# Attention scores as four matmuls of 32 weight columns instead of one of 128, on one core of a Trainium2 chip

## The reference

```python
x = x + ln(attn(ln(x)))                 # 16 heads of 8 features, with a TISA bias
x = x + ln(ffn(ln(x)))                  # msa without bias, then a mixture of 8 experts
# attn: logits = (q @ k.T) / sqrt(8) + bias[head, i - j]; softmax over j; @ v
# ffn:  x = x + msa(ln1(x)) @ w_proj; x = x + expert(argmax gate)(ln2(x))
```

## Time and profile before

| | |
|---|---|
| median of three executions | 914.77 us (913.09 to 916.9) |
| span of the profiled execution | 917.8 us |
| TensorE (PE) matmuls, busy | 810.0 us (88%), 8,629 records |
| weight loads (PEld), busy | 302.8 us (33%), 8,629 records |
| VectorE (DVE), busy | 752.3 us (82%) |
| ScalarE (ACT), busy | 636.7 us (69%) |
| GpSimd (POOL), busy | 242.1 us (26%) |
| scores_a, line 1266 | 1,024 matmuls, mean 394 ns, together 327.5 us busy |
| scores_b, line 1305 | 1,024 matmuls, mean 387 ns, together 333.7 us busy |

### The profile page before, as it was taken

How to read it: one execution, slowest core, us unless ns; L and a number is a source line. 1 busy time by engine, 2 the same in 40 slices (tenths; PEclk the granted TensorE clock), 3 DMA queues, 4 the chain that set the end, 5 groups by cost and what they waited for, 6 DMA issues and landing times.

```text
span 917.8 us, 22092 instructions
## 1 busy us (share of the span) xinstructions
PE 810.0 (88%) x8629; PEld 302.8 (33%) x8629; DVE 752.3 (82%) x1196; ACT 636.7 (69%) x1266; POOL 242.1 (26%) x548
## 2 busy tenths in 40 slices
PE   4269999999999999999999999999999999954960
PEld 2013333333333333343232223322232322344950
DVE  5469978899999998879899998899999899336734
ACT  6027777777777777777678989899988899921311
POOL 4010413201000415222300533333011301004773
PEclk9559999999999999999999999999999999976985
DMA  3654444565555455355313333242322121001313
GB/s 98 186 170 154 133 161 141 157 199 174 171 173 162 142 164 170 125 168 174 100 54 100 109 113 98 65 126 79 93 59 54 54 85 52 28 18 48 52 49 100
DMA packets 69469, 104.67 MB, mean 114 GB/s; under 512 B 15845, under 2 KB 45861, under 8 KB 69365
## 3 DMA queue, kind: packets, MB, share of 16 engines
q1 hardware_dynamic: 62805, 68.31, 25.7%
q10 hardware_dynamic: 5088, 31.92, 10.0%
q0 software_dynamic: 1472, 3.02, 1.5%
HBM read 84.19 MB, written 18.87 MB: 112 GB/s over the span
## 4 chain that ended last, share of the span: by engine, by line
PE 67%; DVE 10%; POOL 6%; DMA 5%; issue 4%; ACT 4%; SPq 3%; ACTq 0%; POOLq 0%; DVEq 0%
PE bank L1286 23%; PE bank L1305 20%; PE bank L1312 11%; PE bank L1266 7%; DVE unit_max L1003 4%; ACT prob_mem L901 3%; POOL prob_mem L791 3%; POOL moe_out L797 2%; DMA maxima_rows<-max_rows 2%; PE bank L1349 2%; PE bank L1239 1%; DVE no_use L999 1%; DVE stats L946 1%; PE bank L1234 1%; DMA k_parts<-prob_mem 1%
## 5 line engine op out<-in xcount | busy, mean ns | idle before, releaser
L901 ACT ACTIVATE prob_mem<-bank 128x512 f32<-128x512 f32 x1024 | 556.6, 597 | 149.3 <-PE bank L1312 124.0
L1266 PE MATMUL bank<-k_rows,q_rows 56*128 56x512 bf16 x1024 | 327.5, 394 | 22.6 <-DMA k_rows<-k_parts 12.3
L1305 PE MATMUL bank<-q_rows,k_rows 59*128 59x512 bf16 x1024 | 333.7, 387 | 12.0 <-DMA k_rows<-k_parts 5.3
L999 DVE CUSTOM_DVE_ANT_1 no_use<-bank,w_moe 128x1024 bf16<-128x1024 f32 x256 | 305.5, 1218 | 37.6 <-PE bank L1266 33.4
L1286 PE MATMUL bank<-prob_mem,v_ring 128*32 128x256 f32 x4096 | 322.2, 388 | 7.7 <-issue 6.6
L1003 DVE TENSOR_REDUCE unit_max<-bank 128x1 f32<-128x1024 f32 x256 | 297.5, 1215 | 19.7 <-PE bank L1266 18.1
L702 POOL CAST max_parts<-unit_max 128x8 bf16<-128x8 f32 x64 | 12.1, 189 | 568.5 <-DVE unit_max L999 321.0
L1305 PEld LDWEIGHTS bank<-q_rows,k_rows 59*128 59x128 bf16 x1024 | 80.8, 93 | 244.0 <-issue 114.7
L1286 PEld LDWEIGHTS bank<-prob_mem,v_ring 128*32 128x32 f32 x4096 | 103.0, 109 | 153.5 <-ACT prob_mem L901 61.8
L1312 PE MATMUL bank<-skew_mem,pick 96*32 96x512 bf16 x1664 | 138.7, 390 | 0.0
L1010 DVE TENSOR_TENSOR bank<-bank,w_moe 128x512 f32<-128x512 f32 x96 | 67.0, 698 | 26.0 <-PE bank L1305 25.8
(11 more groups left out here) (177 smaller groups left out, 525.0 us busy)
## 6 DMA issues: line engine op xcount, KB each, us to landing
w_moe<-bias_rows ACTq DMA_DIRECT2D x31, 960.0 KB, 5.7
q_rows<-q_parts SPq DMA_DIRECT2D x252, 48.0 KB
k_rows<-k_parts SPq DMA_DIRECT2D x126, 96.0 KB
skew_mem<-bias_parts SPq DMA_DIRECT2D x32, 378.0 KB, 4.9
unit_sums<-o_ring SPq DMA_DIRECT2D x63, 128.0 KB, 2.4
w_moe<-in_L_ffn_w_dram SPq DMA_DIRECT2D x16, 256.0 KB, 3.1
q_parts<-prob_mem SPq DMA_DIRECT2D x8, 384.0 KB, 3.1
k_parts<-prob_mem SPq DMA_DIRECT2D x24, 128.0 KB, 2.8
```

The lines of the kernel that those rows point to most:

```text
L901: nc.scalar.activation(prob[:, kb, half * N:(half + 1) * N], b_bank(("exp", exp_no(n, kb, half))), ACT.Exp).then_inc(exp_done, 1)
L999: nc.vector.tensor_tensor_reduce(out=no_use[:, qb % 2, :].rearrange("p (k c) -> p k c", k=QB), in0=scores.rearrange("p (k c) -> p k c", k= ...
L1266: return nc.tensor.matmul(sa_slot(QB * m + qb)[:, f, :], q_rows[rows, m % SLOTS, qb * P:(qb + 1) * P], k_rows[rows, m % SLOTS, f * N:(f + ...
L1305: return nc.tensor.matmul(b_bank(("exp", exp_no(n, kb, f))), k_rows[rows, n % SLOTS, kb * P:(kb + 1) * P], q_rows[rows, n % SLOTS, f * N:( ...
```

## The change

Both score functions loop over four groups of 32 weight columns. Each group has its own matmul, which writes 32 partitions of the same bank and is placed at the tile position (64 f, 32 c). The moving operand is the same 512 columns for all four. Waits and increments stay on the first and last instruction of a half; the order, the banks and the values computed stay.

```diff
--- before.py
+++ after.py
@@ -1263,8 +1263,12 @@
             def scores_a(m, qb, f):
 
                 rows = slice(f * HP, f * HP + KR)
-                return nc.tensor.matmul(sa_slot(QB * m + qb)[:, f, :], q_rows[rows, m % SLOTS, qb * P:(qb + 1) * P],
-                                        k_rows[rows, m % SLOTS, f * N:(f + 1) * N], start=True, stop=True)
+                for c in range(4):
+                    at = qb * P + VM * c
+                    ins = nc.tensor.matmul(sa_slot(QB * m + qb)[VM * c:VM * (c + 1), f, :], q_rows[rows, m % SLOTS, at:at + VM],
+                                           k_rows[rows, m % SLOTS, f * N:(f + 1) * N], start=True, stop=True,
+                                           tile_position=(f * HP, VM * c))
+                return ins
 
             def sa_free(i):
                 if i >= 2:
@@ -1302,9 +1306,13 @@
 
             def scores_b(n, kb, f):
                 rows = slice(f * HP, f * HP + KR + 3)
-                return nc.tensor.matmul(b_bank(("exp", exp_no(n, kb, f))), k_rows[rows, n % SLOTS, kb * P:(kb + 1) * P],
-                                        q_rows[rows, n % SLOTS, f * N:(f + 1) * N],
-                                        start=True, stop=(stage_of(n) == 1 or by_dve(n, kb, f)))
+                for c in range(4):
+                    at = kb * P + VM * c
+                    ins = nc.tensor.matmul(b_bank(("exp", exp_no(n, kb, f)))[VM * c:VM * (c + 1), :], k_rows[rows, n % SLOTS, at:at + VM],
+                                           q_rows[rows, n % SLOTS, f * N:(f + 1) * N],
+                                           start=True, stop=(stage_of(n) == 1 or by_dve(n, kb, f)),
+                                           tile_position=(f * HP, VM * c))
+                return ins
 
             def bias_b(n, kb, f):
                 for c in range(4):
```

## The result

The changed kernel takes 921.66 us (median of four, 919.91 to 923.02) against 914.79 us, ratio 1.0074 with a 95% interval of 1.005 to 1.0098. It is slower by 6.9 us, as forecast in sign (925.5 us, range 916 to 941), and by about two thirds of the amount. Timed once more on another chip, the ratio was 1.0083 (1.0055 to 1.0111). The profiled spans differ by less, 919.0 against 917.8 us, because the clock of the execution profiled before dipped for a moment in two places where the one profiled after kept 1.00: from 720 to 740 us it is 0.91 before and 1.00 after, and from 450 to 460 us 0.83 and 1.00.

A forecast was written before the change was run, and what follows sets the result against it. PE was taken to bound the attention stages, with DVE close behind. Growth left after waits, 32 x 0.22 + 30 x 0.20 = 13 us, less a fifth, gave +10.5 us: 925.5 us, range 916 to 941.

The forecast's parts named there:

- Bound and sign: Attention stages: PE holds 67% of the chain, DVE close behind, so added PE time slows the kernel; slower given 75%.
- Shape changes: Between scores and 32-column tiles in each key block: two gaps of about 0.08 to 0.1 us stay, gain nought.
- Rival 1: Drain hangs on columns, so both gaps of each key block close and DVE sets the limit: 877 us; chance 9%.
- Weight loads and issue: PE's 6,144 extra loads and 6,144 extra matmuls cost nothing, being overlapped and covered by the queue running ahead.
- Rival 4: Eight tiles do not stream together (near 1,130 us), or issue cannot keep up (some 100 us slower); chance 5%.
- Start spacing: Score phase: eight tiles start 3.4 ns apart, filling like the weighting's four f32 tiles; 0.034 us more per key block.
- a sign of being right: Stage 2 key block: second round of scores 0.24 us after the first, weighting still 0.31 after that round's last start.
- Rival 2: Nothing to measure: row groups fill in parallel or waits swallow the rest, 914 to 919 us; chance 14%.
- Rival 3: Slower start spacing, bf16 tiles 7 ns apart: 20 to 38 us after slack, 935 to 953 us; chance 12%.
- What is hidden: Waits PE already has absorb part of each unit's 0.27 us growth: 0.05 in stage 1, 0.07 in stage 2.
- The fifth taken off for busy units: Units where DVE or ACT also serve norms and splits are less bound by PE: 13 us cut to 10.5.

The follow-up runs named there:

- the control: Kernel before, scores in whole 128-column tiles, with stage 2's weighting over 64 of each block's 128 keys; four executions took 914.29 to 1,048.98 us.

## Why the prediction was right, and where it was off

**Bound and sign.** PE's time was the kernel's time, right: 0.02 us on a key block came out as 0.12 to 0.14 on a unit of eight, and as 7 to 9 us on the kernel. Stage 2's busy DVE did not hide it.

**Shape changes, taken at nought.** Right, and now shown from three sides: the gaps stayed, they close with equal shapes, and each half of a mixed pair pays 0.1 us. The rule of the Trainium skill, "TensorEngine Tiling (Array Packing)", Key Properties, that a change of mode drains the engine, agrees with all three. Rival 1 fails. Its other premise held: with the gaps closed, DVE did set the unit, at 9.04 us (I had put 9.2).

**Weight loads and issue, at nothing.** Right: 90 ns a load, 29,546 PE loads and matmuls instead of 17,258, and the loads of a second round begun 0.2 us ahead of it. Eight tiles stream together. Rival 4 fails.

**Start spacing, 0.034 us per key block.** This term was mis-sized: it measured 0.018. The spacing of 3.4 ns was right, and the last tile of a round does start 0.02 later. But I took the weighting's f32 phase as the nearest row and added its later second round (10 to 14 ns). The tiles of the score rounds restart at 0.226 us as before. The second round of scores_b does come 0.24 after its first, which I had named as a sign of being right, but only because its row group now starts 13 ns after the other one and not 3. So the eight blocks of a unit grow by 0.14 us instead of 0.27. Rival 2 fails by this too: the row groups start in line and not in parallel, and 921.66 lies outside its 914 to 919 us. Rival 3 fails, with no spacing near 7 ns.

**What is hidden.** I had 0.05 us a unit in stage 1 and 0.07 in stage 2. With a growth of 0.14, the units grew by 0.13 to 0.14 and by 0.12 to 0.13, so stage 1 hid next to nothing and stage 2 about 0.02. The fifth taken off for busy units was not warranted, since those grew by 0.12 to 0.14 as well. By units the sum is 62 x 0.13 = 8 us.

So 10.5 us came of one term nearly twice too large, in part offset by two deductions that were not there. Without them the same growth would have made 62 x 0.27 = 17 us. That the forecast came within 4 us of the measured time is to this extent luck; that the time lies in the range is not. (914.77 and 10.5 make 925.3; the 925.5 forecast is 0.2 too high.)

**The reason given for the growth** is only half settled. The rows of the changed kernel show the line of eight tiles directly. But the version with two tiles cost the same, and there the line is shorter; as far as these rows go, what splitting the columns costs is the later of the two, line and load, and my theory had only the line.

## What to carry to other kernels

Splitting a matmul into narrower column tiles that stream the same moving columns saves nothing by itself, and lengthens each score phase, here by 0.02 us in a block of 1.11. It can pay only where it makes the whole tile shape, rows and columns, equal to that of the neighbours, because only then does the 0.1 us drain between them go; and before that is counted as a gain, see which engine comes next (here DVE, 0.2 us a unit below) and what the granted clock does (here it fell in parts of stage 2). Don't pair halves of different shapes: they do not run side by side, and the version that paired them throughout ran at half the clock and took 2,014 us in its one execution.

## What the runs showed of the hardware beyond this

- Row groups are served out of program order, with or without the change: scores_a of the second round, last of the four in the program, started before scores_b, as its rows had been taken first (633.61 before 633.62 us; 632.25 before 632.26 in the kernel before, whose records show it in 212 of 239 complete stage 2 blocks).
- PE shown busy without a gap does not tell the clock: it is so for 60.00 of 60 us at 0.50 with mixed pairs and for 40.00 of 40 at 0.50 in the control, while the kernel before has 59.36 of 60 at 1.00. Part of this is an effect of the clock, since each matmul takes longer at 0.50 (0.61 us against 0.39). What lets the clock fall stays open. The same kernel can go either way: with stage 1 alone split, two of seven executions had a mean clock of 0.915 and five one of 0.943 to 0.946.
- A 32-column load is no slower than the 128-column one (90 against 93 ns), a 64-column one takes 104.
